# Gate and up adapter products over 128 rows, and a quarter of the mixed values in the third down tile

## The reference, cut to what matters

```python
def _fused_linear(x, W, qa, qb, scale, w):
    out = x @ W.T
    a = jnp.einsum('th,krh->tkr', x, qa)
    b = jnp.einsum('tkr,khr->tkh', a, qb)
    mix = jnp.einsum('tkh,tk->th', b, w)
    return out + scale[None, :] * mix
...
def expert(muW, gW, gqa, gqb, gs, uW, uqa, uqb, us, dW, dqa, dqb, ds, w):
    xe = x + w @ muW.T
    gate = jax.nn.silu(_fused_linear(xe, gW, gqa, gqb, gs, w))
    up = _fused_linear(xe, uW, uqa, uqb, us, w)
    return _fused_linear(gate * up, dW, dqa, dqb, ds, w)
```

## Time and profile before

| | us |
|---|---|
| median of 3 runs | 1695.51 |
| lowest and highest run | 1692.44 and 1696.01 |
| span of the profiled execution | 1685.8 |
| PE busy | 1568.4 |
| DVE busy | 1155.5 |
| POOL busy | 737.8 |
| ACT busy | 617.2 |

### The profile page before, as it was taken

One profiled execution on the slowest core, in us unless ns is written; L12 is line 12 of the kernel. 1 busy time (PEld: TensorE's weight loads), 2 busy tenths in 40 slices (PEclk: granted clock), 3 DMA queues, 4 the chain that ended last, 5 costly groups with the idle time before them and its releaser, 6 DMA issues.

```text
span 1685.8 us, 19547 instructions
## 1 busy us (share of the span) xinstructions
PE 1568.4 (93%) x6856; PEld 1155.1 (69%) x6856; DVE 1155.5 (69%) x1634; ACT 617.2 (37%) x971; POOL 737.8 (44%) x537
## 2 busy tenths in 40 slices
PE   3787799798888999999999999999999999999999
PEld 2343377566666677777777777777777777777776
DVE  5798964788999867487888755778888553333333
ACT  5545443444454434443343244333433321111111
POOL 4488510489898801077777301376786000000000
PEclk8799999899999999999999999999999999999999
DMA  7688627688787664765667445587665456566552
GB/s 251 215 285 315 254 80 253 201 290 297 270 289 286 253 255 172 248 228 205 232 238 258 152 161 196 202 275 257 238 208 180 175 200 210 184 222 222 195 181 85
DMA packets 111473, 375.87 MB, mean 223 GB/s; under 512 B 20176, under 2 KB 45776, under 8 KB 94864
## 3 DMA queue, kind: packets, MB, share of 16 engines
q1 hardware_dynamic: 101904, 340.81, 57.8%
q10 hardware_dynamic: 9472, 33.82, 5.8%
HBM read 304.33 MB, written 70.25 MB: 222 GB/s over the span
## 4 chain that ended last, share of the span: by engine, by line
PE 63%; DVE 18%; issue 5%; ACT 5%; POOL 4%; DMA 3%; SPq 0%; ACTq 0%; DVEq 0%; POOLq 0%
PE b_g L735 14%; PE b_u L735 14%; PE b_u L826 7%; DVE ring L1493 4%; PE b_g L826 3%; PE b_q L781 3%; PE b_q L826 3%; PE b_g L799 2%; DVE ring L1499 2%; PE b_g L766 2%; DVE tt L1467 2%; POOL ring L1392 2%; PE b_g L759 1%; POOL yx L1401 1%; DVE z L1467 1%
## 5 line engine op out<-in xcount | busy, mean ns | idle before, releaser
L1392 POOL TENSOR_TENSOR ring<-du,rep 128x512 f32<-128x512 f32 x256 | 344.5, 1349 | 151.4 <-DVE du L1571 91.9
L735 PE MATMUL b_g<-xnb,gm 128*128 128x512 f32 (+1 forms) x1440 | 356.2, 396 | 0.9 <-DVE xnb L1470 0.9
L735 PE MATMUL b_u<-xnb,gm 128*128 128x512 f32 (+1 forms) x1440 | 349.1, 391 | 0.0
L1493 DVE TENSOR_TENSOR_SCAN ring<-b_a,ring 128x512 f32<-128x512 f32 x256 | 310.8, 1214 | 15.7 <-ACT b_a L964 8.4
L1401 POOL TENSOR_TENSOR yx<-yx,ring 128x512 f32<-128x512 f32 x192 | 261.8, 1364 | 130.4 <-DVE ring L1499 129.9
L735 PEld LDWEIGHTS b_g<-xnb,gm 128*128 128x128 f32 (+1 forms) x1440 | 252.1, 179 | 89.1 <-issue 24.6
L735 PEld LDWEIGHTS b_u<-xnb,gm 128*128 128x128 f32 (+1 forms) x1440 | 257.1, 179 | 71.1
L1467 DVE SCALAR_TENSOR_TENSOR tt<-tt,b_g 128x512 f32<-128x512 f32 (+1 forms) x120 | 82.1, 684 | 222.7 <-ACT tt L964 222.5
L964 ACT ACTIVATE b_a<-delta,a_neg 128x512 f32<-128x512 f32 x256 | 173.6, 681 | 113.9 <-DVE ring L1493 113.9
L964 ACT ACTIVATE tt<-b_g 128x512 f32<-128x512 f32 (+1 forms) x120 | 71.1, 593 | 316.7 <-PE b_u L766 286.3
L826 PE MATMUL b_u<-dwt,hhl 128*128 128x512 f32 (+1 forms) x720 | 185.4, 394 | 0.0
(11 more groups left out here) (254 smaller groups left out, 2120.2 us busy)
## 6 DMA issues: line engine op xcount, KB each, us to landing
gm<-scr_gm SPq DMA_DIRECT2D x64, 1024.0 KB, 6.8
dwt<-scr_dw SPq DMA_DIRECT2D x32, 1536.0 KB, 6.8
rep<-bc_d ACTq DMA_DIRECT2D x64, 512.0 KB, 5.8
gm<-scr_gm SPq DMA_DIRECT2D x32, 768.0 KB, 4.4
dqt<-scr_dq SPq DMA_DIRECT2D x25, 896.0 KB, 9.1
scr_gm<-gm SPq DMA_DIRECT2D x20, 1024.0 KB, 7.5
scr_dw<-dwt SPq DMA_DIRECT2D x10, 1536.0 KB, 6.2
qat<-scr_qa SPq DMA_DIRECT2D x25, 512.0 KB, 10.2
```

The costliest lines, as they stand in the source:

```text
L735: i = mm(out_b[0:IW[m], :], w, v, start=(n == 0), stop=(n == 11 and not is_routed(s)))
L1392: v.tensor_tensor(ring[:, T % NRING], du[:, T % 4, :], rep[:, N % NREP, 0], ALU.mult).then_inc(pool_dbu, 1)
L1493: v.tensor_tensor_scan(w, ba[T % 2][:], w, 0.0, ALU.mult, ALU.add).then_inc(dve_scan, 1)
```

## The change

In `adapters`, the factors stand in a tile `qbx` of four planes of 128 partitions, and the values in a tile `awt` of four planes, with halves placed so that one product over 128 rows sums two terms: gate takes planes 0 and 2, up takes planes 1 and 3, four products per m in place of eight. Plane 0 of `qbx` holds the high factor of gate in both halves and meets high values in one half and low values in the other; plane 2 holds the low factor in one half and the mask factor in the other. The mask factor for the adapter input has a tile of its own (`gqa`). Copies issued by SP (`aw_load`) place the values in `awt`: two of the mask weights, two of the high values (each into two planes), two of the low values; PE waits for all six. `qb` is loaded in four parts. In batch 0, ACT rounds it in four parts and DVE subtracts in two.

For the down adapter, the low factor of 32 of the values moves into rows 96 to 127 of the third tile of `dwt`, which 96 columns of the inner width leave idle, and ACT writes the rounded values into the same rows of the third tile of `hh`; the other part of the low factor lies in rows of `dqt`. `adapter_b` has one product per row tile in place of two. The order in `routed` changes: row tiles 2 and 3 of the first two inner tiles come right behind `adapter_a`, then the next expert's first gate half (`up(s + 1, 0, 0)`), and then, for each row tile, the third inner tile and the adapter. PE waits for the mixed values before all of these last ones. In batch 0 two copies put the raw rows in place (`dma_pl`). Constants and the router's weights are loaded in four copies in place of two.

The diff, cut:

```diff
             def load(kind, s):
                 free(sp, kind, s)
-                sp.wait_ge(dma_st[kind], 16 * stored_before(kind, s))
+                sp.wait_ge(dma_st[kind], stored(kind) * stored_before(kind, s))
...
+                if kind == "qb":
+                    at = scr[kind][w_index(s)]
+                    both = at[:, 0:I].rearrange("(j p) i -> p j i", j=2)
+                    for rows in (slice(0, HALF), slice(HALF, P)):
+                        sp.dma_start(qbx[rows, 0:2].bitcast(F32), both).then_inc(dma_t[kind], 16)
+                    sp.dma_start(qbx[0:HALF, 2].bitcast(F32), at[0:HALF, I:2 * I]).then_inc(dma_t[kind], 16)
+                    sp.dma_start(qbx[HALF:P, 3].bitcast(F32), at[HALF:P, I:2 * I]).then_inc(dma_t[kind], 16)
+                    return
...
+            def aw_load(s):
+                r, e = rho(s), s % NX - 2
+                wsrc = ws_d[e * NK:(e + 1) * NK].rearrange("k r l -> (k r) l")
+                if r >= 1:
+                    sp.wait_ge(pe_gu, IC * (body_of(r - 1) + 1))
+                sp.dma_start(aw_g[HALF:P].bitcast(F32), wsrc).then_inc(dma_wst2, 16)
+                sp.dma_start(aw_u[0:HALF].bitcast(F32), wsrc).then_inc(dma_wst2, 16)
+                sp.wait_ge(act_aw, r + 1)
+                for rows, g_ in ((slice(0, HALF), 0), (slice(HALF, P), 1)):
+                    sp.dma_start(awt[rows, g_:4:2].bitcast(F32),
+                                 aw_h[rows].bitcast(F32).unsqueeze(1).broadcast_to([HALF, 2, L])).then_inc(dma_awt, 16)
+                sp.wait_ge(dve_awl, r + 1)
+                sp.dma_start(a_g[HALF:P].bitcast(F32), aw[0:HALF]).then_inc(dma_awt, 16)
+                sp.dma_start(a_u[0:HALF].bitcast(F32), aw[HALF:P]).then_inc(dma_awt, 16)
...
-            sp.dma_start(cs[:], cst).then_inc(dma_cst, 16)
-            sp.dma_start(inv_i[:], inv.partition_broadcast(NE)).then_inc(dma_cst, 16)
+            sp.dma_start(cs[:, 0:C_GW], cst[:, 0:C_GW]).then_inc(dma_cst, 16)
+            sp.dma_start(cs[:, C_GW:C_GW + 3], cst[:, C_GX:C_ALL]).then_inc(dma_cst, 16)
+            sp.dma_start(gw, cst[:, C_GW:C_GX].rearrange("p (c n) -> p c n", c=HC)).then_inc(dma_cst, 16)
+            sp.dma_start(inv_i, inv.partition_broadcast(NE)).then_inc(dma_cst, 16)
...
                     w_load(s + 1)
+                    gqa_load(s + 1)
+                    next_pieces(s + 1, ("qa", "gm0", "gm1", "gm2"))
                     gq_load(s + 1)
-                    next_pieces(s + 1, ("qa", "gm0", "gm1", "gm2", "qb"))
+                    next_pieces(s + 1, ("qb",))
+                    aw_load(s + 1)
...
-                for k, (hl_, v) in enumerate(((0, aw_h), (0, aw_l), (1, aw_h))):
-                    for j, out_b in ((0, bg[m]), (1, bu[m])):
-                        rows = slice(j * HALF, (j + 1) * HALF)
-                        i = mm(out_b[0:IW[m], :], qbt[rows, hl_, cols], v[rows, :], start=False, stop=(k == 2))
+                    pe.wait_ge(dma_awt, 64 * (r + 1))
+                for out_b, w, v in ((bg[m], 0, a_g), (bg[m], 2, aw_g), (bu[m], 1, a_u), (bu[m], 3, aw_u)):
+                    i = mm(out_b[0:IW[m], :], qbx[:, w, cols], v, start=False, stop=(w >= 2))
...
                     for v, hl_ in ((hh, 0), (hl, 0), (hh, 1)):
+                        k = slice(0, P if full and v is hh else IW[m])
...
-                mm(down_bank(s, tc)[:], daw_s[:, t], dqt[:, 0, q], start=False, stop=False)
-                mm(down_bank(s, tc)[:], daw_s[:, t], dqt[:, 1, q], start=False, stop=True
-                   ).then_inc(pe_dn, 1)
+                mm(down_bank(s, tc)[:], daw_s[:, t], dqt[:, 0, QA:Q_D], start=False, stop=True).then_inc(pe_dn, 1)
...
-                down(s, 0, (2,))
-                down(s, 1, (2,))
-                down(s, 2)
+                down(s, 2, (0, 1))
+                down(s, 3, (0, 1))
                 if post:
                     xn_transposed(b + 1, (2, 3))
-                down(s, 3)
+                if e < NF - 1:
+                    up_waits(s + 1, 0)
+                    up(s + 1, 0, 0)
+                if 2 < s < NX:
+                    pe.wait_ge(dma_pl, 32 * (s - 2))
+                pe.wait_ge(dve_daw, rho(s) + 1)
+                pe.wait_ge(act_daw, 3 * (rho(s) + 1))
                 for tc in DONE:
+                    down(s, tc, (2,))
                     adapter_b(s, tc)
...
+                if kind == "qb":
+                    rounded(qbx[0:HALF, 0], src[0:HALF, 0:I])
+                    rounded(qbx[HALF:P, 1], src[HALF:P, 0:I])
+                    rounded(qbx[HALF:P, 0], src[0:HALF, 0:I])
+                    rounded(qbx[0:HALF, 1], src[HALF:P, 0:I]).then_inc(act_hi[slot_of[k]], 1)
+                    return
...
-                rounded(rnd[:], dawf[:]).then_inc(act_daw, 1)
+                rounded(daw_s[:], dawf[:]).then_inc(act_daw, 1)
+                rounded(hh[C1, 2], dawf[C1]).then_inc(act_daw, 1)
+                act.wait_ge(act_daw, 3 * rho(s) + 1)
+                rounded(daw_s[C0B], dawf[C0]).then_inc(act_daw, 1)
...
+                if kind == "qb":
+                    src = raw[slot_of[k]]
+                    lo(qbx[0:HALF, 2], src[0:HALF, 0:I], qbx[0:HALF, 0])
+                    lo(qbx[HALF:P, 3], src[HALF:P, 0:I], qbx[HALF:P, 1]).then_inc(lo_done[slot_of[k]], 1)
+                    return
```

More of the change, by code:

```diff
@@ L110, in gated_ssm_moe @@
         xn_h, xn_l = xnb[:, 0], xnb[:, 1]
-        wr, ws = sb("wr", [P, 2, L]), sb("ws", [P, 2, L], F32R)
+        wr = sb("wr", [P, 2, L])
         aw, dawf = sb("aw", [P, L]), sb("dawf", [P, L])
         inv_f = dawf[0:NE, 0:NE]
-        awp = sb("awp", [P, 2, L], F32R)
-        aw_h, aw_l = awp[:, 0], awp[:, 1]
-        rnd, daw_s = sb("rnd", [P, L], F32R), sb("daw_s", [P, L], F32R)
+        awt, aw_h = sb("awt", [P, 4, L], F32R), sb("aw_h", [P, L], F32R)
+        a_g, a_u, aw_g, aw_u = awt[:, 0], awt[:, 1], awt[:, 2], awt[:, 3]
+        wsm = sb("wsm", [P, L], F32R)
+        daw_s = sb("daw_s", [P, L], F32R)
         tt = sb("tt", [P, 2, L])
@@ L210, in gated_ssm_moe @@
         dma_x, dma_mu, dma_mq, act_z0 = (sem(n) for n in ("dma_x", "dma_mu", "dma_mq", "act_z0"))
-        dma_stg, dma_gq, dma_wr, dma_ws = (
-            [sem(n + str(k)) for k in range(2)] for n in ("dma_stg", "dma_gq", "dma_wr", "dma_ws"))
+        dma_stg, dma_wr = ([sem(n + str(k)) for k in range(2)] for n in ("dma_stg", "dma_wr"))
+        dma_gq, dma_gqa, dma_ws, dma_awt, dma_wst2 = (
+            sem(n) for n in ("dma_gq", "dma_gqa", "dma_ws", "dma_awt", "dma_wst2"))
         dma_s0 = [sem("dma_s0_%d" % k) for k in range(4)]
@@ L300, in scaled, with stored, loaded @@
             return 2 * (s - 3) + (1 if kind == "qb" else 2)
+        def stored(kind):
+            return {"qb": 32, "dw": 32, "dq": 80}.get(kind, 16)
+        def loaded(kind):
+            return 64 if kind == "qb" else 16
         def stored_before(kind, s):
@@ L320, in ready @@
             if from_scratch(s):
-                eng.wait_ge(dma_t[kind], 16 * loads(kind, s))
+                eng.wait_ge(dma_t[kind], loaded(kind) * loads(kind, s))
             elif s == 0:
@@ L454, in w_store @@
                 if b > 0:
-                    for k in range(2):
-                        sp.wait_ge(dma_ws[k], 32 * (NF // 2) * b)
+                    sp.wait_ge(dma_ws, 16 * NF * b)
                 else:
@@ L819, in down @@
                 for m in ms:
-                    if tc == 0:
+                    full = m == IC - 1 and is_routed(s)
+                    if tc == 0 and not full:
                         pe.wait_ge(dve_hl, IC * s + m + 1)
                     n = 3 * m
-                    k = slice(0, IW[m])
                     o = m * H
                     for v, hl_ in ((hh, 0), (hl, 0), (hh, 1)):
+                        k = slice(0, P if full and v is hh else IW[m])
                         i = mm(down_bank(s, tc)[:], v[k, m, t], dwt[k, hl_, o:o + H], start=(n == 0),
@@ L1286, in _ @@
             root(0)
-            f(tgf[:], cs[:, C_GF:C_GF + 1], ACT.Tanh).then_inc(set_act, 1)
+            f(tgf[:], cs[:, C_GW + 1:C_GW + 1 + 1], ACT.Tanh).then_inc(set_act, 1)
             in_evac(0, range(HC))
@@ L1694, in aw_first @@
                 dve.wait_ge(pe_qa, r + 1)
+                need(dve, dma_awt, 64 * r)
                 dve.wait_ge(dma_wr[r % 2], 32 * (r // 2 + 1))
```

163 lines of the change are left out of this document (100 added, 63 removed).

## The result

The changed kernel takes 1703.34 us (median of 20 runs) against 1690.62 for the kernel before (20 runs). One of its runs, 2151.61 at a granted clock of 0.652, was disturbed; without it the median is 1702.72 (1691.94 to 1709.98) and the ratio 1.0069, 95% interval 1.0055 to 1.0082. It is slower by 0.7%, where 1.6% faster was forecast. The three runs shown ahead of the prediction (1695.51) were on the slow side of the twenty.

What follows compares the result with a forecast made beforehand. PE was taken to bound batch 3 and ordinary bodies of batches 1 and 2, DVE batch 0; -18.1 - 25.8 + 15.5 + 1.0 = -27.4 us took the span from 1685.8 to 1658.4, time 1668, range 1646 to 1694.

Steps and rivals of the forecast that it cites:

- batch 3 -18.1: Batch 3, bound by PE alone: six bodies at 2.3 us, the first 2.0, the last 2.3, saved.
- batches 1 and 2 -25.8: Eight ordinary bodies save 2.1 us each, fourth bodies 1.2, fifth 0.9, first 0.5, last 1.9.
- batch 0 +15.5: Batch 0: +16.8 us for the split at seven hand-overs, +0.5 at the first expert, -1.8 at the last.
- start +1.0: Kernel start: two more small copies issued ahead of everything else, +1.0 us (0 to 1.5).
- SP's waits in batch 0: SP's queue: raw down loads stand behind two new waits; taken at nothing, up to 3 us per body for the range.
- the prediction's own sign: Stated test: wrong if batch 3 does not shorten, or batch 0 moves by more than 25 us either way.
- PE's slots: PE products in a body: adapters save 1.4 us, down adapter 0.91, together 2.3 where only PE bounds.
- The cover of the placed copies: Copies ahead of PE's adapters: landing in 3 to 5 us, zero exposed; at first experts 4.0 cover, 0.3 to 1.5 exceeded.
- the slower rival: Placed copies land late at the first adapter in 14 bodies of batches 0 to 2; 1700 to 1742 us; chance 0.10.
- The price of the split in batch 0: DVE loses 2.4 us per hand-over (0.5 to 3.4), 1.5 behind ACT and 0.9 subtracting; seven hand-overs, 16.8.
- The moved gate half: Next expert's hoisted gate half on PE keeps the mixed values' cover, 24 slots or 5.4 us; its bank need just met.
- What I gave 0.10 and 0.15 to: Rivals: 0.10, placed copies land late, 1700 to 1742 us; 0.15, batch 0 held by raw loads, 1690.

Runs made afterwards that it cites:

- mixed2: Changed kernel with 64-row adapters in batch 0 and each batch's first expert, SP's order there as in fe_order; 1654.06 us, ratio 0.9792 to before.
- before_split: Kernel before with only the new split's work added in batch 0 (ACT's one copy as four, DVE's one subtraction as two); 1702.98 us, ratio 1.0083.
- split_kept: down_only with the new split's work put back in batch 0 (four ACT copies, two DVE subtractions of 64 rows); 1691.87 us, ratio 1.0023 to before.
- down_only: Changed kernel with gate and up adapters as before, 64 rows at a time, no value copies, old split in batch 0; 1674.96 us, ratio 0.9912 to before.
- qb_one: Changed kernel with batch 0's factors split by one ACT rounding and one DVE subtraction, placed halves left out; 1690.28 us, ratio 0.9994 to before.
- rep_late: fe_order, with ACT's three 512 KB broadcast loads issued only after the copies into awt have landed; 1690.82 us, ratio 1.0003 to before.
- fe_order: Changed kernel; at each batch's first expert SP issues the copies into awt ahead of the third gate/up tile and down adapter loads; 1695.32 us, ratio 1.0027.
- act_queue: Changed kernel; in batch 3's first expert ACT, not SP, issues the four mixed-value copies; one execution, PE's wait there grew from 6.25 to 10.97 us.

## Why the prediction was wrong

The forecast was -27.4 us on the span, and it became +17.9. By the parts of its sum: batch 3 -18.1, measured -8.4 (7.3 - 15.7); batches 1 and 2 -25.8, measured -9.9 (5.1 + 6.0 - 11.0 - 10.0); batch 0 +15.5, measured +33.8 (6.1 + 27.7); start +1.0, measured +2.4. By the prediction's own sign, batch 0 moving by more than 25, it is wrong. Three of its terms failed: the landing of the placed copies at the first experts (24.5 us), SP's waits in batch 0, taken at nothing (about 8 in after), and, in size, the split (20 for 16.8).

- **PE's slots: right, the size a little high.** Adapters 1.4 foreseen, 1.12 measured; down adapter 0.91 and 0.88. A group of new products takes 0.93 (1446.81 to 1447.74 in batch 3) and the twelve behind it 2.78 (until 1450.52), 0.06 over their slots; I had set 0.91 and nothing. The Trainium skill puts row-tiled pairs at up to 2x ("TensorEngine Tiling (Array Packing)", section "Theoretical Speedup"). With the whole 2x the adapters would have given nothing; this kernel's pairs stay below that bound, and full products beat them by 1.12 us a body.
- **The cover of the placed copies: the step that failed at the first experts.** I had the cover, 4.0 us, and a spread of landings, 2.3 to 15.0, and chose 3 to 5 us because the copies go ahead of the down weights. What stands ahead of them I did not list: 768 KB of `gm`, 640 KB of `dq`, the parts of `qb`, and ACT's 1.5 MB in batches 0 to 2. Four waits of 4.0 to 6.25 us, and the lower clock behind them, made 24.5 us in place of 0.3 to 1.5 each; without the copies (mixed2) the same stretches are as long as before. This was the mechanism of the slower rival, but in 4 bodies, not in 14: in the others the split ends early enough, as the sum said.
- **The price of the split in batch 0: right in mechanism, a little low in size.** 16.8 was foreseen, 1.5 of DVE's wait for ACT and 0.9 of subtraction at each of seven hand-overs. In after the waits grew by 12.3 us in all (13.7 from 1.4), 1.8 each, and the subtractions by 7.5 (16.5 from 9.0), 1.1 each: 19.8. The 13.3 of before_split leaves out two roundings that were part of the forecast. I had read the section of the Trainium skill on DVE against GpSimd ("SBUF — State Buffer", section "Who interferes with whom") as a second subtraction that waits for POOL each time, a loss near 3.4 in all seven. 2.8 each was measured, and the subtractions' share of it, 1.1, is near the 0.9 that I had set. The subtractions of 64 rows do spread, from 518 to 2075 ns in before_split, where those of 128 rows went from 511 to 1604.
- **The moved gate half: it moved a wait that I did not look for.** I named the mixed values as what it covers and asked whether `b_g0` is free in time. I did not ask what it had covered: the first residual addition, on which PE's up half waits. The cover is gone in batch 0: 17.1 us of waits in after, 16.4 in split_kept, with the lower clock behind most of them. These waits are where DVE's lateness shows and no price of their own: down_only has the new order and loses nothing in batch 0, and without the hoist 12.4 us of other waits take their place. Here costing it at nothing was luck.
- **SP's waits in batch 0: taken at zero, up to 3 per body.** Between qb_one (+12.9) and down_only (-0.9) lie 13.8 us, 2.0 for each of seven bodies, which go with the copies: raw loads behind SP's waits, or PE's waits for the copies where these stand later. The two costs seem to overlap in after, by some 5 us: there the split costs 20 and the copies the remaining 8. DVE's and PE's lateness would hide part of the late loads; that is argued and not shown. By the runs: without the split 14.8 are won (27.7 - 12.9), without the copies 8.5 (27.7 - 19.2), without both 28.6, each good to some 3 us.
- **The rivals were treated as one or the other.** Late copies, held raw loads and the dear split all came at once. What I gave 0.10 and 0.15 to as separate cases should have stood in the sum.
- **Batches 1 and 2.** The ordinary bodies gain 2.0 except each batch's second expert (0.4 and 0.5), where PE waits for `qat` (the 2.6 us above), whose load lies behind the first expert's burst; the fourth experts gain 0.6 where 1.2 was set, the fifth 0.8 and -0.5 where 0.9 was, presumably since DVE bounds them. These were not tested singly.

What stays open: the start differs by some us between executions that have the same instructions there. Of its +2.4, 0.59 is that the first shared body's products start later (216.21 against 215.62), and 1.82 that the first twelve of them took 4.81 us, in before 2.99, with the same code; in the other runs these twelve took 2.97 to 3.02 or 4.61 to 4.85. Whether the placed copies could be had in batch 0 without cost was not found: neither place in SP's queue did it. And in batch 3's first expert ACT's rounding of the values is done at 1425.05, but DVE's subtraction starts at 1427.83, behind four residual additions; the low copies wait for it. To take it ahead of these additions was not tried.

## What to carry to other kernels

A copy that is added between two engines is priced by what is in flight on the transfer engines at that moment, from every queue, and not by its size or its place in its own queue; list those transfers for the body in which the cover is shortest, since that body decides. When work is moved to cover one wait, ask which wait it covered until now. And a change that pays in one stage and costs in another can be made in the first alone: with the 128-row adapters left out of batch 0 and of three more bodies, and SP's order altered at first experts, the edits went from 0.7% slower to 2.1% faster.

## What the runs showed of the hardware

A wait can cost PE more than its length. Two up halves of batch 0 in after, behind a short and a longer wait for the same residual addition:

```profile
434.65 3.02 PE L815 MATMUL b_u<-xnb,gm 128*128 128x512 f32 x12 [1.46 <-DVE xx L1554]
...
387.98 5.49 PE L815 MATMUL b_u<-xnb,gm 128*128 128x512 f32 x12 [2.92 <-DVE xx L1554]
```

Behind 0.49 and 1.46 us of idle time twelve products took 3.02; behind 2.71 to 3.44 they took 4.32 to 5.49, at a granted clock of 0.50 where the window was read. A wait of 3 us thus cost up to 2.6 more. The idle time just ahead does not decide it alone: the first twelve products of the first shared body stand behind 0.86 us in before and in after and took 2.99 and 4.81, at granted clocks of 1.00 (215.5 to 220.3) and 0.66 (216 to 222).

The copies between partitions landed after 2.2 to 3.7 us when no large load was ahead (rep_late), after 6.0 to 9.2 behind 1.4 MB in the same queue (after), after 6.5 to 8.4 beside 1.5 MB of another queue (fe_order, batch 1), and after 8.7 to 14.3 in a queue of their own beside the same 1.4 MB and the 1.5 MB of down weights in SP's (act_queue):

```profile
DMA to landing us min/median/max: 8.7/11.2/14.3
```
